# B rows turned in 32x32 blocks on VectorE and carried through memory, in a two-layer recurrent block

## What is computed

```python
params = (x @ w_param.T).reshape(b, l, N_HEADS, PARAM_DIM)
dt = softplus(params[..., 0]); a = exp(-dt)
B = params[..., 1:1 + D_STATE]; C = params[..., 1 + D_STATE:]
cs = cumsum(log(a))                                   # inside a chunk
L = where(tril, exp(cs[:, None] - cs[None, :]), 0)
y_diag = (C @ B.T * L) @ X
states = B.T @ (exp(cs[-1] - cs)[:, None] * X)        # per chunk
S_next = exp(cs[-1]) * S + states
y_inter = (C @ S_prev) * exp(cs)
```

## Time and profile before

| | |
|---|---|
| median of 3 runs | 766.62 us (766.07 to 769.03) |
| the profiled execution | 767.01 us, its span 765.3 us |
| PE busy | 735.6 us, 96% of the span |
| PEld busy | 602.7 us, 79% |
| DVE busy | 506.1 us, 66% |
| ACT busy | 325.8 us, 43% |
| POOL busy | 76.1 us, 10% |
| granted TensorE clock, mean | 0.99 |

### The profile page before, as it was taken

The page is one execution under the profiler, slowest core; times in us unless marked ns, Lnnn a source line. Parts: engine busy times, 40 slices in busy tenths (PEclk is TensorE's granted clock), DMA queues, the critical chain, the costliest instruction groups (busy, mean ns, idle before and its releaser), DMA issues.

```text
span 765.3 us, 18468 instructions
## 1 busy us (share of the span) xinstructions
PE 735.6 (96%) x7316; PEld 602.7 (79%) x7316; DVE 506.1 (66%) x1177; ACT 325.8 (43%) x659; POOL 76.1 (10%) x85
## 2 busy tenths in 40 slices
PE   4888999999999999999999999999999999999997
PEld 3666678877888788887888878888778878888686
DVE  3877679737797367945678467874679737795143
ACT  1312565126642366214752057512664236631570
POOL 6201011001011011000110001100011101100020
PEclk9879999999999999999999999999999999999999
DMA  8800320015000150002400032000500015000220
GB/s 291 318 1 15 116 39 3 1 30 153 2 3 1 44 139 2 3 2 71 112 2 2 3 121 60 3 1 30 147 8 3 0 44 140 2 3 1 96 57 15
DMA packets 33938, 39.77 MB, mean 52 GB/s; under 512 B 20352, under 2 KB 27968, under 8 KB 32192
## 3 DMA queue, kind: packets, MB, share of 16 engines
q1 hardware_dynamic: 33856, 38.49, 16.8%
HBM read 32.12 MB, written 6.36 MB: 50 GB/s over the span
## 4 chain that ended last, share of the span: by engine, by line
PE 93%; DVE 4%; issue 1%; ACT 1%; DMA 0%; POOL 0%; DVEq 0%; SPq 0%; ACTq 0%; POOLq 0%
PE psum L1275 72%; PE psum L1364 4%; PE psum L1474 2%; PE psum L1459 2%; PE psum L1324 1%; PE psum L1335 1%; PE psum L1485 1%; PE psum L1683 1%; PE psum L1512 1%; PE psum L1610 1%; PE psum L1384 1%; PE psum L1556 1%; PE psum L1420 1%; PE psum L1403 1%; PE psum L1427 1%
## 5 line engine op out<-in xcount | busy, mean ns | idle before, releaser
L520 ACT ACTIVATE BC<-psum 64x256 f32<-64x256 f32 x128 | 81.2, 634 | 3.5 <-PE psum L1275 1.8
L1275 PE MATMUL psum<-xnT,sb_f_gate 128*128 128x256 f32 x256 | 66.6, 404 | 1.8 <-issue 1.0
L1275 PE MATMUL psum<-xnT,sb_f_up 128*128 128x256 f32 x256 | 62.3, 385 | 0.0
L1275 PE MATMUL psum<-xn1T,sb_n_gate 128*128 128x256 f32 x256 | 61.4, 383 | 0.0
L1275 PE MATMUL psum<-xn1T,sb_n_up 128*128 128x256 f32 x256 | 60.5, 379 | 0.0
L1275 PEld LDWEIGHTS psum<-xnT,sb_f_gate 128*128 128x128 f32 x256 | 48.7, 198 | 11.6 <-issue 2.9
L1275 PEld LDWEIGHTS psum<-xn1T,sb_n_up 128*128 128x128 f32 x256 | 48.6, 190 | 6.6
L1275 PEld LDWEIGHTS psum<-xn1T,sb_n_gate 128*128 128x128 f32 x256 | 47.3, 190 | 6.5
L1275 PEld LDWEIGHTS psum<-xnT,sb_f_up 128*128 128x128 f32 x256 | 47.1, 189 | 6.6 <-issue 0.2
L868 DVE TENSOR_TENSOR kT<-kT,dec 128x256 f32<-128x256 f32 x56 | 25.2, 450 | 39.3 <-PE psum L1364 31.8
L1275 PE MATMUL psum<-sb_n_down,hidB 128*128 128x256 f32 x224 | 49.5, 379 | 0.0
(11 more groups left out here) (203 smaller groups left out, 1496.4 us busy)
## 6 DMA issues: line engine op xcount, KB each, us to landing
cs_row<-cs_dram SPq DMA_DIRECT2D x8, 1024.0 KB, 5.2
x_dram<-gate SPq DMA_DIRECT2D x8, 512.0 KB, 2.8
cs_half<-cs_dram SPq DMA_DIRECT2D x16, 256.0 KB, 6.3
hidB<-x_dram SPq DMA_DIRECT2D x8, 512.0 KB, 7.9
X<-in_x SPq DMA_DIRECT2D x9, 256.0 KB, 2.8
x<-in_x SPq DMA_DIRECT2D x8, 256.0 KB, 2.7
out_tokens<-thFB SPq DMA_DIRECT2D x8, 256.0 KB, 2.2
sb_w_rkvgo<-in_w_rkvgo SPq DMA_DIRECT2D x1, 1280.0 KB, 5.7
```

The lines of the kernel that those rows point to most:

```text
L520: ins = a_.activation(cols[:, par, 2 * pair:2 * pair + 2, :], src[64 * par:64 * par + 64, :, s, :], ACT.Identity)
L1275: ins = t_.matmul(ps(t, name)[first_row:first_row + rows, col:col + n], w, x, start=(k == 0), stop=(k == len(ws) - 1))
```

## The change

1. The PE transposes of B and of the sums go, and with them the fills `bt0` and `bt1` (the later fills of those two banks move up by one; in the last round the ring of banks shifts by two).
2. B is turned by two VectorE transposes of 32x32 blocks (`B_by_block`, 128x512 each) into `B_turned`. Four DMAs write it to `b_dram` so that each position has its 64 numbers together, and one DMA reads it back into `Brow`, as `Xrow` is read. `states` now waits for `B_decayed` by the semaphore `B_ready`, and `B_decayed` works in place in SBUF.
3. The sums by position (`cs_pos`) are read straight from `cs_dram`, each number by itself, in the place of `cs16`.
4. In the loop `end_args` moves up to between level steps 2 and 3. `end_exp` and `L_exps(0)` move ahead of `res_tanhs`, `L_exps(1)` ahead of `sums_exp`. The sparse counts and selection move back.
5. In the last round `B_by_block` and `end_args` stand between `hidden_n(b, 1)` and `res_gate`.

```diff
-         ["xT1", "csum", "C1", "bt0", "sc1", "ys1", "n1u", "n3u"],
-         ["dt", "B0", "res0", "bt1", "sc3", "n0g", "n2g", "s1"],
+         ["xT1", "csum", "C1", "sc1", "ys1", "n1u", "n3u"],
+         ["dt", "B0", "res0", "sc3", "n0g", "n2g", "s1"],
...
+        B_turned = sb("B_turned", [P, SEQ_T * SH])
-        cs16 = sb("cs16", [NQ * SCH, P])
+        cs_pos = sb("cs_pos", [P, NQ * SCH])
...
-                    sp_.dma_start(cs16[:, :], cs_dram.rearrange("(c p) -> c p", p=P)).then_inc(cs_loaded, 16)
                     sp_.dma_start(flat(cs_row), cs_dram.partition_broadcast(P)).then_inc(cs_loaded, 16)
+                    sp_.dma_start(cs_pos[:, :], cs_dram.rearrange("(c p) -> p c", p=P),
+                                  allow_slow_non_contiguous=True).then_inc(cs_loaded, 16)
...
+                    wait(B_rows, b.count(16, 16))
+                    wait(B_blocks, b.count(2, 2))
+                    to = b_dram.rearrange("(s n i e d) -> s e i n d", s=NQ, i=32, e=2, d=32)
+                    for s in range(NQ):
+                        for e in range(2):
+                            r = 64 * s + 32 * e
+                            sp_.dma_start(to[s, e], B_turned[r:r + 32, :].rearrange("p (n d) -> p n d", d=32)).then_inc(
+                                B_stored, 16)
+                    wait(B_stored, b.count(64, 64))
+                    sp_.dma_start(Brow.rearrange("p q c d -> p (q c) d"),
+                                  b_dram.rearrange("(c p d) -> p c d", p=P, d=SD)).then_inc(B_rows, 16)
...
@@ ACT, loop round
                     gate_tanh()
+                    end_exp()
+                    L_exps(0)
                     act.wait_ge(X_stored, b.count(16, 32))
...
+                    L_exps(1)
                     sums_exp()
-                    end_exp()
-                    L_exps(0)
-                    L_exps(1)
...
+                def B_by_block(half):
+                    wait_freed(dve, b, "B0")
+                    dve.sem_inc(passed, 1)
+                    wait_freed(dve, b, "B1")
+                    n = slice(half * SEQ_T * SH // 2, (half + 1) * SEQ_T * SH // 2)
+                    d.transpose(B_turned[:, n], BC[:, 0, :, :].rearrange("p t h -> p (t h)")[:, n]).then_inc(B_blocks, 1)
...
@@ DVE, loop round
                     level_step(a, 2)
+                    end_args()
+                    B_by_block(0)
+                    level_step(a, 3)
+                    B_by_block(1)
+                    level_step(a, 4)
                     sparse_compare(a, 0, 1)
                     sparse_compare(a, 0, 2)
-                    level_step(a, 3)
-                    sparse_sums()
-                    level_step(a, 4)
-                    sparse_rest()
                     level_step(a, 5)
...
                     res_gate(1)
-                    end_args()
+                    sparse_count()
...
                     B_decayed()
-                    sparse_select(0)
                     decayed_scores(0)
                     hidden_p(a, 3)
                     decayed_scores(1)
                     states_1()
+                    sparse_select(0)
                     compare(1)
+                    gated_1()
                     sparse_count()
-                    gated_1()
                     sparse_select(1)
...
@@ PE, loop round (the last round likewise)
                     keys_turned()
-                    turned_sums()
-                    turned_B()
                     scores(0)
```

More of the change, by code:

```diff
@@ L71 @@
 LAST_FILLS = ["xT1", "dtT", "X0", "X1", "dt", "csum", "B0", "B1", "C0", "C1", "n0g", "n0u", "n1g", "n1u", "res0", "res1",
-              "bt0", "bt1", "sc0", "sc2", "sc1", "sc3", "n2g", "n2u", "st", "n3g", "n3u", "ys0", "ys1", "F1",
+              "sc0", "sc2", "sc1", "sc3", "n2g", "n2u", "st", "n3g", "n3u", "ys0", "ys1", "F1",
               "s1"]
@@ L122, in build_block @@
         W = {n: sb("sb_" + n, list(A[n].shape)) for n in A
-             if n not in ("x", "out", "cs_dram", "x_dram", "w_mix2b", "w_dec2")}
+             if n not in ("x", "out", "cs_dram", "b_dram", "x_dram", "w_mix2b", "w_dec2")}
         W["w_mix2b"], W["w_dec2"] = sb("sb_mix2b", [NQ * DMIX, C]), sb("sb_dec2", [NQ * DDEC, C])
@@ L274, in build_block @@
         X_rows = sem("X_rows")
+        B_blocks = sem("B_blocks")
+        B_stored = sem("B_stored")
+        B_rows = sem("B_rows")
+        B_ready = sem("B_ready")
         res_tanh = sem("res_tanh")
@@ L323, in block_decay @@
             return dec[:, BLOCKS[s]:BLOCKS[s] + CH * T // s]
-        cs_dram, x_dram = A["cs_dram"], A["x_dram"]
+        cs_dram, x_dram, b_dram = A["cs_dram"], A["x_dram"], A["b_dram"]
         def rounds(eng, one):
@@ L393, in one @@
                         out_stored, 16)
-            for s in (X_rows, X_stored, cs_stored, cs_loaded, out_stored):
+            for s in (X_rows, X_stored, cs_stored, cs_loaded, B_rows, out_stored):
                 sp_.sem_inc(s, 16)
@@ L1075, in end_args @@
                 def end_args():
-                    wait_filled(dve, b, "bt0")
-                    did(d.tensor_scalar(cs_col[:, :], ps(b, "bt0")[:, sums_at], -1.0, None, ALU.mult))
+                    dve.wait_ge(cs_loaded, b.count(64, 80))
+                    did(d.tensor_scalar(cs_col[:, :], cs_pos[:, :], -1.0, None, ALU.mult))
                     after()
@@ L1080, in end_args @@
                     d.tensor_tensor(to_end[:, :], cs_row[:, :, P - 1], cs_col[:, :], ALU.add).then_inc(end_arg, 1)
+                def B_by_block(half):
[4 more added lines that the diff above has]
+                    d.transpose(B_turned[:, n], BC[:, 0, :, :].rearrange("p t h -> p (t h)")[:, n]).then_inc(B_blocks, 1)
                 def B_decayed():
                     dve.wait_ge(to_end_ready, b.count(1, 1))
+                    dve.wait_ge(B_rows, b.count(16, 32))
                     for s in range(NQ):
-                        wait_filled(dve, b, f"bt{s}")
-                        free(d.tensor_tensor(Brow[:, s, 0:SCH - 1, :],
-                                             ps(b, f"bt{s}")[:, 0:(SCH - 1) * SD].rearrange("p (c d) -> p c d", d=SD),
-                                             to_end[:, s * SCH:(s + 1) * SCH - 1].unsqueeze(2).to_broadcast(
-                                                 [P, SCH - 1, SD]), ALU.mult), b, f"bt{s}")
+                        B = Brow[:, s, 0:SCH - 1, :]
+                        ins = d.tensor_tensor(B, B, to_end[:, s * SCH:(s + 1) * SCH - 1].unsqueeze(2).to_broadcast(
+                            [P, SCH - 1, SD]), ALU.mult)
+                        if s < NQ - 1:
+                            did(ins)
+                    ins.then_inc(B_ready, 1)
                 def decayed_scores(part):
@@ L1652, in carries @@
                                          [prefix[:, :].rearrange("p (q h) -> p q h", h=SH)[:, :, SH - 1]])])
-                def turned_sums():
-                    pe.wait_ge(cs_loaded, b.count(64, 80))
-                    open_bank(b, "bt0")
-                    pe.sem_inc(passed, 1)
-                    t_.transpose(ps(b, "bt0")[:, sums_at], cs16[:, :], ident[0:NQ * SCH, 0:NQ * SCH])
-                def turned_B():
-                    wait_freed(pe, b, "B1")
-                    open_bank(b, "bt1")
-                    pe.sem_inc(passed, 1)
-                    for c in range(SCH - 1):
-                        for s in range(NQ):
-                            r = half_rows(s)
-                            ins = t_.transpose(ps(b, f"bt{s}")[:, c * SD:(c + 1) * SD], Bf[r, c * P:(c + 1) * P],
-                                               ident[r, r])
-                            if c == SCH - 2:
-                                close_bank(ins, b, f"bt{s}")
                 def scores(part):
@@ L1677, in states @@
                     pe.wait_ge(X_rows, b.count(16, 32))
+                    pe.wait_ge(B_ready, b.count(1, 1))
                     open_bank(b, "st")
-                    for s in range(NQ):
-                        wait_freed(pe, b, f"bt{s}")
+                    pe.sem_inc(passed, 1)
                     for c in range(SCH - 1):
@@ L1895 @@
     aps["cs_dram"] = nc.dram_tensor("cs_dram", (T * SH,), F32).ap()
+    aps["b_dram"] = nc.dram_tensor("b_dram", (T * SH * SD,), F32).ap()
     aps["x_dram"] = nc.dram_tensor("x_dram", (T * SH * SD,), F32).ap()
```

1 line of the change is left out of this document (removed).

## The result

| | before | after |
|---|---|---|
| median | 766.49 us (766.07 to 769.03, 4 runs) | 771.24 us (770.96 to 773.07, 4 runs) |
| ratio to before | | 1.0063, 95% interval [1.0034, 1.0091] |
| span of the profiled execution | 765.3 us | 769.0 us |

The change makes the kernel slower by 0.63%, 4.75 us. The forecast was 766.5 us and "within 0.5%": the time lies inside the range that was given, but on the other side of the bound, and by a mechanism that the prediction does not have.

The account below looks back on a forecast made before the run. PE, busy for 96% of the span, was taken to bound the kernel. Seven loop rounds gaining 7.4 us and a last round losing 7.3 gave -0.1 us, so 766.5 us, with a range of 763.3 to 779.8.

Parts of the forecast that it names:

- PE in the loop: Loop: removed transposes save PE 0.65 us a round; with the 0.51 us gap closed, 1.06 us a round.
- the limit: Loop: B's trip through memory may take 12.2 us before PE's L1474 is delayed; it fits by 0.6 us.
- The trip of B: Loop: from the second turn's end through store and load to B's arrival, 11.6 us.
- the other estimate: VectorE turn priced from the Trainium skill's page at 1.2 us instead of 0.69; 767.6 us in all.
- The likeliest rival: Loop: 128-byte writes cost 30 ns or more a piece, trip 14.2 us, DVE and PE wait; 783 us, chance 0.22.
- The ends of the range: Shortest and longest duration given for B's store and load through memory: 8.4 and 13.8 us.
- The last round: Last round: nothing covers B's store and load, so PE idles ahead of `states`: +7.3 us net.
- the prediction's own formula: Time change by trip R: -7.4 + (R - 4.3) up to 12.2 us, then 8 us more for each us.
- The sums by position ... Free: Loop: the `cs_pos` load takes 2.6 us and delays POOL's mask to 285, before `end_args` asks at 288.5; no cost.
- The rival on `cs_pos`: Loop: over 57 ns a piece, `end_args` holds level step 3 and PE; 806 us at 100 ns, chance 0.05.
- This is the part that can close PE's gap: Loop, DVE: `sparse_select(0)`, 1.42 us, leaves the stretch between `B_decayed` and the scores, against PE's 0.51 us gap.
- A small wait eats part of the gain: Loop: tight banks and the later sparse selection leave 0.3 us gain a round; 771.8 us, chance 0.15.

Follow-up runs that it names:

- Both repairs: Changed kernel, with POOL's mask waiting for cs_row's load alone and the last round's turns of B moved ahead of hidden_n(0): 758.49 us, ratio 0.9905.
- the kernel before with an early mask: Kernel before the change, with POOL's mask waiting for the row's load alone by its own semaphore: 766.35 us, ratio 0.9995.
- first experiment: Changed kernel, with POOL's mask waiting for cs_row's load alone instead of all four loads of the sums: 765.72 us, ratio 0.9984.
- product held back: Both repairs with the sparse choice back between B_decayed and decayed_scores, and POOL's cs_half product waiting until that choice is done: 763.93 us, ratio 0.9966.
- choice put back: Both repairs, with the sparse row's choice put back between B_decayed and decayed_scores: 782.56 us, ratio 1.0216.
- store twice: Both repairs, with the four stores of turned B issued a second time before the load may go: 792.68 us, ratio 1.0349.
- exponentials: Both repairs, with ScalarE's exponentials in their old order, sums ahead of end and the two L exponentials: 765.94 us, ratio 0.9986.
- both orders put back: Both repairs, with the sparse choice's place and the order of the exponentials both as before the change: 771.63 us, ratio 1.0069.

## Why the prediction was right or wrong

**PE in the loop, and the limit: right.** Both repairs against the kernel before with an early mask give 1.13 us a round; 1.06 were predicted. The gap ahead of L1474 is closed, and PE reaches L1502 with about 0.7 us in DVE's hand, as the limit had it (0.6).

**The trip of B: mechanism right, size somewhat too large.** 9.4 us against 11.6 in the round shown. The store took 5.5 us to the load's issue for 6.7, the load 3.8 for 4.9, and a turn 0.70 us as priced, not the 1.2 of the other estimate. The store's leg varies, though: 5.4 to 6.4 us over the loop rounds of the changed kernel and up to 6.9 with both repairs, where the trip so comes to some 10.7 us. There is not much room: DVE asks 11.5 us after the second turn. The likeliest rival (0.22) needed more than 12.2 us, and no loop round of these two had that. The ends of the range, 8.4 and 13.8, don't follow from the terms as given, which add up to 8.9 and 13.4; nothing hangs on this.

**The last round: +7.3 forecast, +6.8 measured, and near by luck.** Two errors cancel: the trip was 9.3 us and not 11.6, which by the prediction's own formula gives +5.0, just what lies ahead of `states`; and the low clock behind the hole, +1.8, was left out.

**"The sums by position ... Free": the step that failed.** It followed the late mask along semaphores only: who waits for it (`L_exps`, `end_args` at 288.5), and found all of them later. No semaphore joins the mask to L868. Still the mask, held back by `cs_pos`, meets that operation, and this gives back 6.5 of the 8.5 us that the loop had gained (first experiment), while the same load in the kernel before costs 8.8 us. The rows for it were there: the mask at 280.46 to 282.46 ended just as L868 began, at 282.44 in that round, and in some rounds before the change L868 took up to 1.01 us. The rival on `cs_pos` (0.05) put the decision at 57 ns a piece, when `end_args` would be held up. It was decided already by a mask 1.1 us late, less than the 2.5 us by which the prediction itself let the mask come later.

**"This is the part that can close PE's gap": right, but two meetings were not seen.** The choice had to leave: at its old place and without any meeting it costs 5.4 us (product held back), and the loop then gains 0.25 us a round in place of 1.13. What the prediction does not have is that `B_decayed`, with its source now in SBUF, meets POOL's product in the old order of the exponentials (7.4 us), and that in their new order the same product meets the choice at its old place (24 us, 18.6 of which go when the product is held back). The two moves together keep both operations apart from the product, and without them the trip of B is a loss of 5 us.

**The rival that named the number.** "A small wait eats part of the gain" (0.15) ends at 771.8 us, and 771.24 were measured. This is luck: it had the loop at -2.1 us from small waits at two banks and at the sparse selection. The loop did come to -2.0, but as -8.5 and +6.5, and no row shows such a small wait; with both repairs PE is idle for 0.4 us in the whole loop.

**The sum.** -8.5 (loop, first experiment against before) + 6.5 (meeting) + 5.0 (hole) + 1.8 (clock) = +4.8 us, against +4.75 of the medians. Forecast without the meeting, with the measured trip: about 764 us; without hole and meeting the kernel runs in 758.5.

## What to carry to other kernels

Before moving anything on one of two engines that share a path to memory, lay their timelines over each other and list which pairs now overlap: it is not a dependency, so neither the waits nor the order shows it, only a duration that is longer than that of its group. A late transfer is not free because its own reader is later; follow whatever it delays to what that lies over. And a hole in TensorE can cost more than itself: behind some of the holes of 2 us and more the products ran at a lower clock, behind others of the same length they did not, so the slower products belong in the range of a forecast.

## What the runs showed of the hardware

- DVE and POOL exclude each other by whole instructions where the DVE operation has both inputs in SBUF. Seen with four kinds: the level step's `kT` (0.43 us alone, up to 1.87 beside the mask in the changed kernel and up to 2.23 with the scattered load in the kernel before), its `rT` (0.42, up to 2.22), `B_decayed` (1.15, 2.17 beside POOL's product) and the choice (1.43 and 3.57). The blocked operation of the level step ends 0.26 to 0.29 us after POOL's instruction. It works the other way too: where the level step began 0.05 us first, the mask took 2.24 us in place of 2.00. `decayed_scores`, with one input in PSUM, keeps its 1.28 us under POOL's product (304.06 to 306.43 in the profile after), and so did `B_decayed` its 1.15 while it read PSUM. The Trainium skill, "SBUF — State Buffer", section "Who interferes with whom", says this: the pair of ports that the two share is an exclusive lock, taken by a DVE instruction with two SBUF inputs against a GpSimd instruction that reads SBUF. The trace agrees, and this is the rule that spoke against the change.
- A load of 8 KB in 2048 pieces of 4 bytes makes the next issues slow: the two `cs_half` issues took 1.11 us before and 4.08 us behind `cs_pos` in the round shown (4.04 to 4.53 us over the rounds).
- 512 KB written in 4096 pieces of 128 bytes took 5.3 to 6.3 us in the changed kernel's loop from the first of the four issues to the issue of the load that waits for all of them, against 2.8 us to landing for the same bytes of X. With all issuing and landing in it, that is 21 to 25 ns a piece and DMA engine, under the 30 ns of the rival.
- A hole in PE can be followed by a stretch at the lower clock, but its length alone did not tell when. Of the 14 holes of 2.1 to 3.4 us in two versions (choice put back, store twice) six were followed by a granted clock of 0.63 to 0.79 over the 8 us from the next product and eight by 1.00; holes of 2.27 us are in both groups. Behind the hole of 5.6 us in the last round it was 0.50, the lower level, at first. Behind holes of 0.9 to 1.4 us (exponentials or both orders put back) it stayed at 1.00, the upper level, in all 14 rounds. What decides was not found.
